# The last row work of the second feed-forward inside its last group, two slots for the quantiser's tiles, and earlier loads of the first weights

## What is computed

```
x = x + _layernorm(_L0_attn_ref(_layernorm(x), Wq, Wk, Wv, Wo))
x = x + _layernorm(_L0_ffn_ref(_layernorm(x), w_gate, w_up, w_down))
x = x + _layernorm(_L1_attn_ref(_layernorm(x), ...))
x = x + _layernorm(_L1_ffn_ref(_layernorm(x), w_gate_up, w_proj))
```

## Time and profile before

| | us |
|---|---|
| median of 3 runs | 3284.5 (3283.2 to 3285.5) |
| profiled execution, its own time | 3277.8 |
| its span, first to last instruction | 3275.9 |
| PE busy | 2868.3 (88%) |
| DVE busy | 1893.0 (58%) |
| ACT busy | 1196.3 (37%) |
| POOL busy | 997.4 (30%) |
| mean granted PE clock | 0.937 of full speed |
| f0f, first DMA issue to last matmul | 720.5 to about 1341 |
| f1f, first DMA issue to last addition | 2849.1 to 3225.0 |
| f1s and f1r | 3225.6 to the end |

### The profile page before, as it was taken

The page is one execution under the profiler, slowest core; times in us unless marked ns, Lnnn a source line. Parts: engine busy times, 40 slices in busy tenths (PEclk is TensorE's granted clock), DMA queues, the critical chain, the costliest instruction groups (busy, mean ns, idle before and its releaser), DMA issues. The chain is left out here.

```text
span 3275.9 us, 42814 instructions
## 1 busy us (share of the span) xinstructions
PE 2868.3 (88%) x14636; PEld 2291.9 (70%) x14636; DVE 1893.0 (58%) x3638; ACT 1196.3 (37%) x2327; POOL 997.4 (30%) x784
## 2 busy tenths in 40 slices
PE   7969999769899999558899999777999999399994
PEld 6846666548677777437788888666888887288883
DVE  5647888474343444445566666654666666544445
ACT  2226666422112212133344444333444444233331
POOL 1227778644444546304100000132000000222223
PEclk9969999879999999779999999989999999699997
DMA  4774444131121101671100000120000000300002
GB/s 167 236 212 127 128 135 127 47 113 54 51 71 46 55 25 41 181 294 68 39 23 34 22 22 34 52 113 28 24 33 22 34 22 18 132 14 16 19 1 103
DMA packets 138035, 244.06 MB, mean 75 GB/s; under 512 B 14417, under 2 KB 78929, under 8 KB 137393
## 3 DMA queue, kind: packets, MB, share of 16 engines
q1 hardware_dynamic: 137904, 242.40, 22.7%
HBM read 162.92 MB, written 79.17 MB: 74 GB/s over the span
## 5 line engine op out<-in xcount | busy, mean ns | idle before, releaser
L1067 POOL TENSOR_TENSOR l0a_probs_hl<-l0a_probs,l0a_probs_hl 128x896 fp32r<-128x896 f32 (+1 forms) x128 | 284.9, 2245 | 107.9 <-ACT l0a_probs L995 107.9
L1299 PE MATMUL l1a_obank<-l1a_pT_hl,l1k_v_hl 128*128 128x512 f32 (+3 forms) x1152 | 300.3, 370 | 7.2 <-DVE l1a_pT_hl L1372 7.1
L1325 ACT ACTIVATE l1a_probs<-l1a_scores,l1a_row 128x128 f32<-128x128 f32 (+7 forms) x256 | 189.3, 740 | 317.3 <-DVE l1a_row L1362 317.3
L1372 DVE TENSOR_TENSOR l1a_pT_hl<-l1a_work,l1a_pT_hl 128x512 fp32r<-128x512 f32 (+3 forms) x384 | 212.9, 555 | 154.1 <-ACT l1a_pT_hl L1332 153.9
L1415 POOL TENSOR_TENSOR l1a_q_stage<-l1k_qpe,l1a_ones 128x512 fp32r<-128x512 f32 x32 | 33.3, 1040 | 872.8 <-PE l1a_work L1307 816.9
L1279 PE MATMUL l1a_scores<-l1k_kT_hl,l1a_qa_hl 128*128 128x512 f32 (+3 forms) x1152 | 291.0, 361 | 1.5 <-ACT l1a_probs L1325 1.5
L1629 PE MATMUL f0f_ybank<-f0f_wT,f0f_h_hl 128*128 128x512 f32 x768 | 201.8, 415 | 36.0 <-POOL f0f_h_hl L1745 35.9
L1332 ACT CAST l1a_pT_hl<-l1a_work 128x512 fp32r<-128x512 f32 (+3 forms) x384 | 183.6, 478 | 105.9 <-PE l1a_work L1290 104.7
L1307 PE MATMUL l1a_work<-l1a_wov,l1a_oT_hl 128*128 128x512 f32 x768 | 214.3, 402 | 5.0 <-DVE l1a_oT_hl L1391 3.0
L1362 DVE TENSOR_REDUCE l1a_row<-l1a_scores 128x1 f32<-128x128 f32 (+7 forms) x256 | 189.7, 750 | 44.2 <-PE l1a_scores L1282 44.0
L1386 DVE SCALAR_TENSOR_TENSOR l_acc<-l1a_work,l1a_row,l_acc 128x512 f32<-128x512 f32 x256 | 189.3, 750 | 34.4 <-PE l1a_work L1307 25.0
(11 more groups left out here) (255 smaller groups left out, 6186.2 us busy)
## 6 DMA issues: line engine op xcount, KB each, us to landing
v_dram<-l0f_v_rows SPq DMA_DIRECT2D x24, 768.0 KB, 4.2
qk_dram<-l0f_stage SPq DMA_DIRECT2D x128, 128.0 KB, 2.5
l1a_wov<-wov_dram SPq DMA_DIRECT2D x32, 512.0 KB, 3.4
l0a_v_stage<-v_dram SPq DMA_DIRECT2D x32, 384.0 KB, 4.4
l1a_wabs<-wabs_dram SPq DMA_DIRECT2D x32, 384.0 KB, 3.8
l0a_q_stack<-qk_dram SPq DMA_DIRECT2D x32, 256.0 KB, 3.6
l0a_k_stack<-qk_dram SPq DMA_DIRECT2D x32, 256.0 KB, 3.9
f0f_chunk<-in_L_ffn_w_gate_up SPq DMA_DIRECT2D x32, 256.0 KB, 2.8
```

The source lines that it names most:

```text
L1067: nc.gpsimd.tensor_tensor(probs_hl[:, r, 1, 0:wide], probs[:, r, 0:wide], f32(probs_hl[:, r, 0, 0:wide]), ALU.subtract).then_inc(low_done, 1)
L1299: last = pe.matmul(obank[:, c:SPAN], src["v_hl"][:, a, n, :], pT_hl[:, ring(n, s), b, c:SPAN], start=(n == 0 and i == 0), stop=(n == QT * ...
L1325: nc.scalar.activation(probs[s][:, first:first + wide, :].rearrange("p k c -> p (k c)"), scores[:, n % S_AHEAD, 0:wide * P], ACT.Exp, bias ...
L1372: nc.vector.tensor_tensor(pT_hl[:, r, 1, c:SPAN], work[:, slot, c:SPAN], f32(pT_hl[:, r, 0, c:SPAN]), ALU.subtract).then_inc(work_free[slo ...
```

## The change

1. The first two groups of weights of each feed-forward are loaded a phase earlier: in l0o behind its first two row loads, and in f1n behind the row loads. `raw` is allocated outside the feed-forward for that, and the feed-forward's SP only raises `loaded`.
2. In f0f, `chunk` and `quant` have two slots each. SP loads chunk c when cast c - 2 has been done, and stores chunk c - 5 behind it.
3. DVE's wait for the cleared `acc` stands before its first addition.
4. f1s and f1r are gone. In f1f's last group, new events do that work span by span: R, four row sums of squares on PE; S, statistics of one tile of `acc` on DVE; V, the variance with the row's own epsilon (the factor per row is folded into it: the normalisation of a scaled row is that of the row with another epsilon); Q, its root on ACT; I, reciprocal and shift on DVE; Z, the normalised tile on ACT (Identity with scale and bias), the addition of the row on POOL, and on DVE for the last span. SP loads the rows and stores the results.

```diff
+            for tile, extra in loads:
+                sp.dma_start(tile, extra).then_inc(next_loaded, 16)
...
+def finish_events(u, step):
+
+    if step == 0:
+        return [("S", u, 0, t) for t in range(QT // HT)]
+    return [("S", u, 0, t) for t in range(QT // HT, QT)] + [("V", u, 0, 0), ("Q", u, 0, 0), ("I", u, 0, 0)]
...
+            if finish and sp >= 1 and ht == HT - 1:
+                ev.append(("R", sp - 1, 0, 0))
             ev += beside("C") + [("K", half, sp, ht)] + beside("MEL")
+            if finish and sp >= 1:
+                if sp >= 2:
+                    ev += [("Z", sp - 2, 0, t) for t in range(ht * QT // HT, (ht + 1) * QT // HT)]
+                ev += finish_events(sp - 1, ht)
+    if finish:
+        u = SPANS - 1
+        ev += [("D", half, u, 0), ("D", half, u, 1)]
+        ev += [("Z", u - 1, 0, t) for t in range(QT)] + finish_events(u, 0)
+        ev += [("D", half, u, t) for t in range(QT // HT, QT)] + [("R", u, 0, 0)] + finish_events(u, 1) + [("Z", u, 0, t) for t in range(QT)]
+        return ev
...
+def group_loads(raw, g, half, gate, up, down):
+
+    pairs = [(raw[:, half, w, :].rearrange("p (h d) -> p h d", h=HT),
+              src[bass.ds(g * HG, HG), :].rearrange("(h p) d -> p h d", p=P)) for w, src in ((0, gate), (1, up))]
+    return pairs + [(raw[:, half, 2, :].rearrange("p (o c) -> p o c", o=KT),
+                     down[:, bass.ds(g * HG, HG)].rearrange("(o p) c -> p o c", p=P))]
...
+        def load(g, half):
+            sp.wait_ge(w_full, WBANKS * (g - 1))
+            for dst, src in group_loads(raw, g, half, gate, up, down):
+                sp.dma_start(dst, src).then_inc(loaded[half], 16)
+
         def load_chunk(c):
-            wait(sp, cast_done, c)
-            sp.dma_start(chunk[:, :], chunks[c][0]).then_inc(chunk_loaded, 16)
+            wait(sp, cast_done, c - 1)
+            sp.dma_start(chunk[:, c % 2, :], chunks[c][0]).then_inc(chunk_loaded[c % 2], 16)
 
         def store_chunk(c):
             sp.wait_ge(quant_done, c + 1 + WB)
-            sp.dma_start(chunks[c][1], quant[:, :]).then_inc(quant_stored, 16)
-
-        load(0, 0, False)
-        load(1, 1, False)
+            sp.dma_start(chunks[c][1], quant[:, c % 2, :]).then_inc(quant_stored[c % 2], 16)
...
+        for half in range(2):
+            sp.sem_inc(loaded[half], 48)
...
+                def load_rows(u):
+                    wait(sp, sum_done, QT * (u - 1))
+                    sp.dma_start(x[:, u % 2], src[u * SPAN:(u + 1) * SPAN, :].rearrange("(t p) d -> p t d", p=P)
+                                 ).then_inc(x_loaded[u % 2], 16)
+
+                load_rows(0)
+                load_rows(1)
+                for u in range(SPANS):
+                    for t in range(QT):
+                        if u < SPANS - 1:
+                            sp.wait_ge(sum_done, u * QT + t + 1)
+                        else:
+                            sp.wait_ge(sum_last, t + 1)
+                        n = u * QT + t
+                        sp.dma_start(dst[n * P:(n + 1) * P, :], z[:, t, :]).then_inc(row_stored[t], 16)
+                    if u + 2 < SPANS:
+                        load_rows(u + 2)
+                for t in range(QT):
+                    sp.wait_ge(row_stored[t], 16 * SPANS)
...
                     load_chunk(c)
-                    if c >= 3:
-                        store_chunk(c - 3)
+                    if c >= 5:
+                        store_chunk(c - 5)
                     if g < NG and c == first + 2:
-                        load(g, g % 2, True)
-            for c in range(len(chunks) - 3, len(chunks)):
+                        load(g, g % 2)
+            for c in range(len(chunks) - 5, len(chunks)):
...
+                elif kind == "R":
+                    pe.wait_ge(sq_added, seen["K"] + 1)
+                    pe.wait_ge(w_read, NG * WBANKS + 2)
+                    pe.wait_ge(ones_set, 2)
+                    wait(pe, var_done, half - 1)
+                    for t in range(QT):
+                        tok = (half * QT + t) * P
+                        last = pe.matmul(row_sums(half)[:, t:t + 1], squares[:, tok:tok + P], ones[:, :],
+                                         start=True, stop=True)
+                    last.then_inc(summed, 1)
...
+                elif kind == "Q":
+                    act.wait_ge(var_done, half + 1)
+                    nc.scalar.activation(root[:, half % 2, :], var[:, half % 2, :], ACT.Sqrt, bias=eps2[:, 0:1]
+                                         ).then_inc(root_done, 1)
+                elif kind == "Z":
+                    act.wait_ge(shift_done, half + 1)
+                    wait(act, row_stored[b], 16 * half)
+                    nc.scalar.activation(z[:, b, :], acc[:, half * QT + b, :], ACT.Identity,
+                                         bias=shift[:, half % 2, b:b + 1], scale=rstd[:, half % 2, b:b + 1]
+                                         ).then_inc(z_done, 1)
...
-        dve.wait_ge(zeroed, 1)
...
+                    if isinstance(it, int) and it == 0 and half == 0 and a == 0 and b == 0:
+                        dve.wait_ge(zeroed, 1)
...
+                elif kind == "S":
+                    par = half % 2
+                    dve.wait_ge(y_read, seen["D"] + 2)
+                    nc.vector.bn_stats(stats[:, par, b, :], acc[:, half * QT + b, :]).then_inc(stats_done, 1)
+                    dve.wait_ge(stats_done, seen["S"] + 1)
+                    nc.vector.bn_aggr(mv[:, par, b, :], stats[:, par, b, :]).then_inc(mv_done, 1)
+                elif kind == "V":
+                    par = half % 2
+                    dve.wait_ge(summed, half + 1)
+                    dve.wait_ge(mv_done, QT * (half + 1))
+                    nc.vector.scalar_tensor_tensor(out=var[:, par, :], in0=row_sums(half), scalar=EPS_LN / HID,
+                                                   in1=mv[:, par, :, 1], op0=ALU.mult, op1=ALU.add).then_inc(var_done, 1)
+                elif kind == "I":
+                    par = half % 2
+                    dve.wait_ge(root_done, half + 1)
+                    wait(dve, z_done, QT * (half - 1))
+                    nc.vector.reciprocal(rstd[:, par, :], root[:, par, :]).then_inc(rstd_done, 1)
+                    dve.wait_ge(rstd_done, half + 1)
+                    nc.vector.scalar_tensor_tensor(out=shift[:, par, :], in0=mv[:, par, :, 0], scalar=-1.0,
+                                                   in1=rstd[:, par, :], op0=ALU.mult, op1=ALU.mult
+                                                   ).then_inc(shift_done, 1)
+                elif kind == "Z" and half == SPANS - 1:
+                    dve.wait_ge(z_done, seen["Z"] + 1)
+                    dve.wait_ge(x_loaded[half % 2], 16 * (half // 2 + 1))
+                    nc.vector.tensor_tensor(z[:, b, :], z[:, b, :], x[:, half % 2, b, :], ALU.add).then_inc(sum_last, 1)
...
+                    pool.wait_ge(quant_stored[b % 2], 8 * seen["M"] + (16 - 8 * (b % 2)))
+                    nc.gpsimd.tensor_tensor(quant[:, b % 2, :], wb[:, b % WB, :], r, ALU.add).then_inc(quant_done, 1)
+                elif kind == "Z" and half < SPANS - 1:
+                    pool.wait_ge(z_done, seen["Z"] + 1)
+                    pool.wait_ge(x_loaded[half % 2], 16 * (half // 2 + 1))
+                    nc.gpsimd.tensor_tensor(z[:, b, :], z[:, b, :], x[:, half % 2, b, :], ALU.add).then_inc(sum_done, 1)
```

More of the change, by code:

```diff
@@ L1493, in feed_forward @@
     WC = KT * HG
-    raw = m.sb("raw", [P, 2, 3, WC], F32 if ternary is None else BF16)
     wT = m.sb("wT", [P, 2, PARTS, 3, WC], F32R)
@@ L2282, in two_layers @@
                 xT0 = after.sb("xT0", [P, 2, KT, NT * P], F32R, side="right")
+                raw0 = after.sb("raw0", [P, 2, 3, KT * HG], side="right")
+                ffn0 = [a[f"L0_ffn_w_{n}"] for n in ("gate", "up", "down")]
                 WoT = keep.sb("WoT", [P, 2, 1, KT, D], F32R)
```

131 lines of the change are left out of this document (55 added, 76 removed).

## The result

The changed kernel takes 3201.8 us (median of 4 runs, 3199.9 to 3203.3) against 3283.9 us on the same chip before: a ratio of 0.975, 95% interval 0.9733 to 0.9767, so 82 us or 2.5% faster. The prediction said 3203, with 3191 to 3228 as its range. The profiled execution took 3199.93 us, with a span of 3198.2 us where it was 3275.9: 77.7 us to be found, where 81.5 were forecast.

A forecast was written before the change was run, and what follows sets the result against it. TensorE, busy 88% of the span, bounds the kernel, so its idle places count. Savings of 8.4 + 4.6 + 30.3 + 38.2 = 81.5 us take 3277.8 to 3196.3 profiled, 3203 as median; range 3191 to 3228.

The forecast's parts named there:

- f0f starts earlier, 8.4 us: Start of the first feed-forward: with weights loaded a phase earlier, it begins at 720.6 instead of 729.04, 8.4 us gained.
- f1f, 4.6 us: Start of the last feed-forward: with weights loaded earlier, it begins at 2849.3 instead of 2853.92, 4.6 us gained.
- The moved loads, 0 us: In l0o and f1n: the early weight loads cost nothing there; 0 to 3 us if their cover fails.
- Two slots, 30.3 us: In f0f: second slots for chunk and quant remove long and last-turn waits and the slowed matmuls behind them, 30.3 us.
- The idle term of 23.3: In f0f: TensorE's 35.9 us of idle less three turn beginnings of 4.2 us leaves 23.3 us removed.
- The three waits stay, 5.6 us each: At turn beginnings in f0f: three waits for a stored chunk remain, costing about 5.6 us each.
- The end, 38.2 us: End of f1f: row work interleaved with the last group moves the end from 3275.9 to 3237.7, 38.2 us gained.
- What would show it: Signs listed for the profile after; one, at f1f's end, was about 19 us from the last low half to the end.
- POOL stays just inside: End of f1f: span 2's additions and a 2.2 us store finish at 3232.9, before the last slot is wanted at 3233.1.
- Identity without a table load: In f1f's last group: Identity needs no table load; the rival with its own table or late engines had 15%, 3213 us.
- the waits at a turn's beginning go too: Rival, 5%: f0f's three turn-beginning waits vanish as well, 17 us more gained, 3186 us.
- DVE or ACT late: Rival in f1f's last group, 15% with Identity needing its own table: engines run late between spans, 10 us back, 3213.

The follow-up runs named there:

- the second profile: The changed kernel run and profiled again with nothing altered, on the chip of two later runs: 3203.4 us, 0.976 of before.
- the better version: The changed kernel with the store of the chunk five behind issued ahead of a chunk's load: 3180.5 us, 0.9704 of before.
- another order: The kernel before, one slot each, with a group's three weight loads issued one chunk later, between chunk load and store: 3260.5 us, 0.9948.

## Why the prediction was right

The forecast's mechanism held in every part, and the sum was 3.8 us too high in the profiled execution. By its own steps:

- **f0f starts earlier, 8.4 us.** From POOL's start to the first H 8.9 us were gained and 1.3 given back by slower first matmuls. "Nothing else is late there" was right in order and not in clock: the prediction did not ask at which clock the first H would run. The wait for the cleared accumulator, taken at nothing, hides behind two H steps as said; at its old place it would have cost 4.0 us.
- **f1f, 4.6 us:** 4.9 measured, 5.1 when undone, of which 0.7 is given back inside f1f (358.0 us from H to H without the early loads, 358.7 with them). The prediction had no term for that.
- **The moved loads, 0 us:** confirmed in both phases (f1n, first x load to POOL's start in f1f: 36.0 us after, 35.9 before). If the cover is gone, 2.4 us, inside the 0 to 3.
- **Two slots, 30.3 us:** 29.1 in the experiment that undoes them. In the changed kernel the segment is 28.4 shorter, 1.3 of it less because the first H's slow matmuls fall inside it. The idle term of 23.3 came out as 23.4 (35.9 less 12.5). What the text credited to chunk and quant together belongs to chunk alone.
- **The three waits stay, 5.6 us each:** they stayed, 12.5 us idle and 6.1 slow, 6.2 each. The prediction named the store's place in SP's program as the cause; exchanging two lines took all three away.
- **The end, 38.2 us:** 37.9 from the last H, but 2.4 were lost ahead of it where 1.8 of row sums were counted, and those 1.8 are already in the 38.2; so the right comparison is 35.5, 2.7 too few. Of these, 1.3 lie behind the last low half (17.0 us to the end, where 15.7 were worked out; the 19 under "What would show it" does not follow from that working), 0.7 between the last H and that low half, whose last pass took 1.35 us and not 0.89, and 0.6 ahead of the last H, where the end undone puts 1.9 us on the row work, and the 0.7 above is of the size of the rest. Row sums took 0.95, not 0.9, each (and its step of 5.44 us reads POOL's addition as 1.29 where the earlier trace rows has 1.27, on which nothing hangs). The Identity was mis-sized: four in 2.93 us, where 2.3 were taken from the square's row. The last span's passes also waited 1.02 us for a stored row in this execution. "POOL stays just inside" looked at the last slot with 2.2 us for a store (its 3230.3 and 2.2 make 3232.5, not 3232.9); what was late was the first slot, whose store took 5.1 us. In the second profile no store was waited for, but there the last matmuls were slower and the slot was asked for 1.07 us later.
- **Identity without a table load:** the trace shows none before it, in any of its sixteen passes. The loads in the last group are the five that were forecast. That identity needs no load of its own is what the Trainium skill's page "ScalarE: Activation LUTs", section "Table sets", says, and no row before could show it. The Trainium skill's figure of about 2.7 us in that section includes a drain: its section "What ACT_TABLE_LOAD costs", on the same page, has about 1.28 us for the load alone. The load agrees (1.28 us in both kernels); the drain does not show: from the end of a root at 3171.16 to the start of the next Silu at 3172.47 it is 1.31 us, with the load between them. So the prediction's "differs" holds of the whole switch, not of the load.

The sum of the profile was 77.7 and not 81.5: 2.7 too few at the end, 1.9 in f0f, and 0.8 too many at the starts and between. The medians differ by 82.1. The prediction carried its saving over to a median 6.7 us above the profiled execution; after the change that distance is 1.8 us (3201.8 against 3199.9). The profiled execution was the fastest of the four. This luck made 3203 look more exact than its terms were: they were 3.8 us too generous, the distance 4.9 us too wide.

Of the rivals, "the waits at a turn's beginning go too" did not come with this change, and its condition (the store of chunk 9 ahead of the first cast of the next turn) is what the better version fulfils. "DVE or ACT late" did not come: VectorE waits 1.53 us for a Silu behind a table load, twice, and TensorE does not idle ahead of the last span.

## What to carry to other kernels

In an in-order DMA queue, write down for every issue which wait stands ahead of it: here two exchanged lines gave 19.4 us inside f0f (21 in the median) that two more slots had not, and the same place of the store with one slot fewer lost 10 there (11 in the median). A second slot pays only if the store or load that frees it is issued before the wait that needs it. And when a wait at a phase's start is removed, move the next one too (the cleared accumulator, 4.0 us), and ask at what clock the work then runs.

## What the runs showed of the hardware

The clock at f0f's start was not expected. Windows of 1 us of TensorE in the changed kernel (length, busy, clock, DMA share, GB/s):

```profile
726.00:727.00 1.00, 0.61 (x5) 1.00 0.00 0
...
728.00:729.00 1.00, 0.00 (x0) 0.81 0.00 0
729.00:730.00 1.00, 0.94 (x2) 0.50 0.00 0
...
732.00:733.00 1.00, 1.00 (x5) 0.98 0.00 0
```

While the weights were turned the clock had risen to 2.4 GHz (1.00). It fell back to 1.2 GHz (0.50) about the 1.40 us that TensorE waits ahead of the first H, stayed there for three microseconds of dense work, and was back by 733. With the store ahead of the load it did not rise while the weights were turned (0.50 in every window from 720 to 732), and the first H was as slow, 4.48 us. With the early loads undone, it rises late in the turning and stays:

```profile
732.00:736.00 4.00, 2.43 (x12) 0.68 0.02 7
736.00:741.00 5.00, 4.61 (x20) 1.00 0.00 0
```

All kernels that idle 11.5 us before the turning or 5.5 us in it run their first H in 3.07 us, and all that idle 3.2 us before it need 4.4 to 4.9. Why is open.

The length of a short idle stretch alone does not tell what the matmuls behind it cost. In f0f, 1.87 us made twelve of them 4.60 us, but 2.26 us two steps earlier in the same execution left them at 3.01, and with another order 2.07 us left 3.00 and 1.79 us made 4.36:

```profile
1286.50 3.01 PE L1629 MATMUL f0f_ybank<-f0f_wT,f0f_h_hl 128*128 128x512 f32 x12 [2.26 <-POOL f0f_h_hl L1745]
```

At the end of f1f, 1.60 us of idle time left eight down matmuls at 2.14 us in the first profile of the changed kernel, and 1.61 us made them 2.63 and the next eight 3.78 in the second.

An Identity that takes scale and bias per row for 128x512 takes 0.80 us, one every 0.73, against 0.63 for a square of that size.
